# Second half of the query transposes moved within a turn: ahead of the last two gate/up groups and the tanh

## What is computed

```
x = x + tanh(g_xattn) * mlstm(q=layernorm(x), k=ctx, v=ctx)      # 16 heads of 64, scans of log gates
n = layernorm(x)
x = x + tanh(g_ffn) * (shared(n) + routed(n))                    # 16 experts, the best 2 of each token
shared(n) = (silu(n @ sg) * (n @ su)) @ sd
```

## Time and profile before

| | us |
|---|---|
| median of 3 runs | 2925.34 |
| lowest and highest run | 2923.26, 2928.15 |
| the profiled execution: its span, from the first to the last instruction | 2941.0 |

### The profile page before, as it was taken

How to read it: one execution, slowest core, us unless ns; L and a number is a source line. 1 busy time by engine, 2 the same in 40 slices (tenths; PEclk the granted TensorE clock), 3 DMA queues, 4 the chain that set the end, 5 groups by cost and what they waited for, 6 DMA issues and landing times.

```text
span 2941.0 us, 49274 instructions
## 1 busy us (share of the span) xinstructions
PE 2784.3 (95%) x17322; PEld 2290.3 (78%) x17323; DVE 1845.4 (63%) x2800; ACT 1015.8 (35%) x1948; POOL 996.6 (34%) x1148
## 2 busy tenths in 40 slices
PE   3799999999999986999999999999999999999999
PEld 2677777777777774788888888888888888888887
DVE  3787878878887854454555545545545546767676
ACT  4445444444444421233333333333333331111111
POOL 1334433434344423343343443443443411111111
PEclk7799999999999997999999999999999999999999
DMA  6445545554555541344444444443443327666665
GB/s 196 148 158 170 159 141 162 166 153 152 162 169 159 145 166 65 136 150 150 145 150 148 146 153 144 146 153 143 148 152 143 100 108 213 182 203 183 203 182 182
DMA packets 243470, 458.24 MB, mean 156 GB/s; under 512 B 99696, under 2 KB 131824, under 8 KB 240624
## 3 DMA queue, kind: packets, MB, share of 16 engines
q1 hardware_dynamic: 116976, 333.62, 33.9%
q0 software_dynamic: 34880, 73.10, 8.1%
q10 hardware_dynamic: 91488, 49.82, 6.3%
HBM read 358.96 MB, written 115.31 MB: 161 GB/s over the span
## 4 chain that ended last, share of the span: by engine, by line
PE 59%; DVE 1%; issue 0%; ACT 0%; DMA 0%; SPq 0%; ACTq 0%; DVEq 0%
PE p_g_b L1608 19%; PE p_up_b L1608 19%; PE p_y_b L1594 19%; PE p_h_b L1581 1%; DVE x_t_b L1473 0%; DVE w_lo L1439 0%; DMA xn<-mid_xn 0%; ACT w_hi L1361 0%; SPq L1204 0%; DVE xt_lo_b L1479 0%; ACT xt_hi_b L1394 0%; DVE th_b L1485 0%; DVE x L1515 0%; DVE x L1506 0%; DVE y_b L1517 0%
## 5 line engine op out<-in xcount | busy, mean ns | idle before, releaser
L1300 POOL DMA_INDIRECT xn<-mid_xn,idx_q x284 | 304.5, 1072 | 512.6 <-DVE x_t_b L1473 424.6
L1608 PE MATMUL p_g_b<-w_hi,xt_hi_b 128*128 128x512 f32 x840 | 334.6, 398 | 19.8 <-DVE xt_lo_b L1479 16.9
L1594 PE MATMUL p_y_b<-w_hi,ht_hi_b 128*128 128x512 f32 x840 | 327.4, 390 | 1.9 <-DVE ht_lo_b L1462 1.9
L1608 PE MATMUL p_g_b<-w_lo,xt_hi_b 128*128 128x512 f32 x840 | 328.6, 391 | 0.0
L1608 PE MATMUL p_g_b<-w_hi,xt_lo_b 128*128 128x512 f32 x840 | 328.4, 391 | 0.0
L1608 PE MATMUL p_up_b<-w_hi,xt_lo_b 128*128 128x512 f32 x840 | 328.0, 390 | 0.0
L1608 PE MATMUL p_up_b<-w_hi,xt_hi_b 128*128 128x512 f32 x840 | 327.8, 390 | 0.0
L1608 PE MATMUL p_up_b<-w_lo,xt_hi_b 128*128 128x512 f32 x840 | 327.7, 390 | 0.0
L1594 PE MATMUL p_y_b<-w_hi,ht_lo_b 128*128 128x512 f32 x840 | 327.5, 390 | 0.0
L1594 PE MATMUL p_y_b<-w_lo,ht_hi_b 128*128 128x512 f32 x840 | 327.4, 390 | 0.0
L1462 DVE TENSOR_TENSOR ht_lo_b<-p_h_b,ht_hi_b 128x512 fp32r<-128x512 f32 x74 | 51.0, 690 | 367.5 <-ACT ht_hi_b L1377 367.5
(11 more groups left out here) (224 smaller groups left out, 5585.8 us busy)
## 6 DMA issues: line engine op xcount, KB each, us to landing
mid_y<-y_b SPq DMA_DIRECT2D x73, 512.0 KB, 2.6
stage<-mid_g_row SPq DMA_DIRECT2D x64, 512.0 KB, 5.4
stage<-in_eg SPq DMA_DIRECT2D x16, 2048.0 KB
stage<-in_eu SPq DMA_DIRECT2D x16, 2048.0 KB
stage<-in_ed SPq DMA_DIRECT2D x16, 2048.0 KB
mid_y<-in_x SPq DMA_DIRECT2D x34, 512.0 KB
stage<-in_x SPq DMA_DIRECT2D x32, 512.0 KB
stage<-in_ctx_t ACTq DMA_DIRECT2D x32, 512.0 KB, 8.9
```

Of the source, the lines that this page charges most:

```text
L1300: nc.gpsimd.indirect_dma_start(out=xg_parts[:, n, :], out_offset=None, in_=xn_flat, in_offset=bass.IndirectOffsetOnAxis(ap=idx_q[:, n:n + ...
L1594: last = nc.tensor.matmul(p_y[n][:, :], a[:, k, :], b[:, GUP + k, w], start=(k == 0 and m == 0), stop=(k == FE // P - 1 and m == 2))
L1608: mm = nc.tensor.matmul(out[:, :], a[:, k, :], w[:, k, o:o + FE], start=(k == 0 and m == 0), stop=(k == KD - 1 and m == 2))
```

## The change

The step Q3 moves from the end of the tuple to the place between Z1 and U1. PE thus transposes the second half of the queries ahead of K7 and K8, and ACT copies it ahead of the tanh. Offsets, waits, tiles and all other steps stay as they are; the order of the steps that share `p_tr` among each other is the same.

```diff
                 "A9", "F2", "B4", "A7", "A8", "E3", "G2", "R1", "G3", "C1", "F3", "G4", "X1", "G5", "Q2", "C2", "G6",
-                "E4", "W6", "Z1", "U1", "D1", "K7", "K8", "Q3")
+                "E4", "W6", "Z1", "Q3", "U1", "D1", "K7", "K8")
```

## The result

| | median, us | lowest to highest | runs |
|---|---|---|---|
| before, beside the changed kernel | 2926.74 | 2923.26 to 2930.46 | 4 |
| after | 2941.71 | 2938.29 to 2943.12 | 4 |

The change makes the kernel slower: ratio 1.0048, 95% interval 1.0036 to 1.0060. The prediction, 2922.5 us with a range of 2909 to 2938, was wrong in sign and the time lies outside the range. It lies where the third rival put it (2939.9).

A forecast was written before the change was run, and what follows sets the result against it. PE, busy 95% of the span, was taken to bound the kernel. Terms -17.4 + 1.1 + 13.5 = -2.8 us, put on the runs' median of 2925.34 us, gave 2922.5 us, range 2909 to 2938.

The forecast's parts named there:

- the third rival: PE stops ahead of K7 for Q2's copy, DVE meets POOL just as often: +14.6 us, 2939.9 us; chance 0.20.
- The 17.4 us of irregular waits: PE's 19 waits for DVE at L988, L981 and L1044 in turns 2 to 29, all taken as going: -17.4 us.
- undisturbed turns: PE waits at A3 instead of A2 and is 0.04 us later at B2: +1.1 us over 28 turns.
- stops at L943: Ahead of K7, Q3's transposes wait for ACT's copy of Q2, which shares their PSUM buffer: 19 turns, +13.5 us.
- The gap at A2 isn't saved, it goes to A3: A2 starts earlier, but A3 needs L707 from the DVE chain: some 0.7 us wait there replaces 0.8 us at A2.
- B2 0.04 us later per turn: The second half of L1044 follows the second L762 and starts at 533.06 instead of 533.02 in turn 14.
- A new wait for ACT's copy: Q3's transposes at L943 wait for ACT's copy of Q2, up to 1.3 us each in 19 turns: 13.5 us.
- the slow side: Signs of a too low forecast: L943's waits add up to over 20 us, or L988's and L1044's stay at 11 us.
- The irregular waits go: The later DVE chain passes its collisions with POOL, so waits at L988, L981 and L1044 vanish: -17.4 us, the softest term.
- The first: Rival: the regular gap ahead of A2 is simply saved, 28 x 1.06 = 29.7 us, 2895.6 us; chance 0.06.
- The second, 2909 us: Rival: the irregular waits go and Q2's copy is in time, -16.3 us, 2909.0 us; chance 0.14.

The follow-up runs named there:

- the second profile of before: The kernel before, unedited, profiled anew on the same chip as the kernel after: 2925.58 us, profiled span 2925.1 us.
- the second profile of after: The kernel after, unedited, run on the same chip as the kernel before: 2938.85 us, 1.0044 times before.
- The kernel with the buffer: Order of the change, but Q3's transposes go into one of the two score buffers: 2929.83 us (0.9997 of before), on another chip 2928.68 us (0.9994).
- the trace of after that ran beside the buffer: The changed kernel, unedited, on the same chip as the second run with Q3's own buffer: 2937.77 us, 1.0028 of before.

## Why the prediction was wrong

The step that failed is the one that put the sum on the median: "the runs' median, 2925.34 us, is 15.7 us lower, and I put the difference on the median". The 17.4 us of irregular waits, taken as all going, were most of what made the profiled execution of before 15.7 us longer than the runs: the second profile of before has 12.9 us less of them, and 26 of its turns take 15.5 us less. That execution, which takes the usual time, has 4.5 us of them, so there the change has little to take away. On the median the term of -17.4 us was worth -3.9.

The account can be made from the starts of the tanh (L630) in turns 2 and 28, 26 turns apart, for the second profile of before:

```profile
136.49 0.60 ACT L630 ACTIVATE th<-p_g 128x512 f32<-128x512 f32 x1 [3.93 <-PE p_up L1006]
...
969.42 0.60 ACT L630 ACTIVATE th<-p_g 128x512 f32<-128x512 f32 x1 [1.98 <-PE p_up L1006]
```

and for after:

```profile
134.54 0.60 ACT L630 ACTIVATE th<-p_g 128x512 f32<-128x512 f32 x1 [2.07 <-PE p_up L1006]
...
980.50 0.60 ACT L630 ACTIVATE th<-p_g 128x512 f32<-128x512 f32 x1 [2.08 <-PE p_up L1006]
```

832.93 and 845.96 us: 13.0 us longer (845.75 us in the second profile of after, from the same chip as this one of before). The turns repeat in fours. Undisturbed ones are 31.51, 31.25, 32.66 and 32.29 us long before, and 31.68, 31.42, 32.89 and 32.45 us after. Turns with a stop, or with a wait at L988, are longer than their kind, and the excess is the price of the disturbance:

| over 26 turns, us | predicted (28 turns) | measured, against the usual execution of before |
|---|---|---|
| undisturbed turns | +1.1 | (31.68 + 31.42 + 32.89 + 32.45 - 127.71) / 4 x 26 = +4.7 |
| stops at L943 | +13.5 | +12.3, in 7 turns, of which 8.5 is idle time |
| irregular waits of before | -17.4 | -3.9, in 4 turns |
| sum | -2.8 | +13.1 |

In the first profile of before the same 26 turns take 848.4 us (134.98 to 983.36), 15.5 us more than in the second, so against that execution after is 2.4 us shorter; the sum said 2.8. The sum was thus about right for the execution that it was made on and wrong for the median. The prediction showed that gap of 15.7 us and even called the irregular waits its softest term, but it doubted whether the change would remove them, not whether the runs had them.

Step by step:

- *The gap at A2 isn't saved, it goes to A3.* Right: 28 waits of 0.75 us, predicted "some 0.7".
- *B2 0.04 us later per turn.* Right in sign, mis-sized: 0.15 us in turn 14, 0.18 us per turn. The prediction let B2's second half follow the second L762, 0.05 us behind its end, the step that it had read between L707 and L981. In the rows of after it is B2's first half that is held, and it starts 0.21 us behind the end of the first L762.
- *A new wait for ACT's copy, 13.5 us in 19 turns, with nothing to cover it.* The mechanism is right, and the runs with and without a shared buffer show it. The total came out near (12.3 us), its parts didn't. There are 7 stops, not 19 (8 and 9 in other profiles). A reading of this, which no run tests, is that a stop sets PE back against ACT, so that the turn behind it finds the copy in time: in after no stop follows directly on another, but in its second profile three do (turns 16 to 18). Instead one stop is long, 3.45 us against "up to 1.3", and costs 2.35 us more by the clock, so that the total is near by luck. L943's waits stayed under the 20 us that were to show the slow side.
- *The irregular waits go.* They are gone in after, as said, but there were few to go, and that the shift of 0.36 us takes them away isn't shown. The kernel with the buffer has the same shift without the stops, and its L989, which is L988 there, waits 4.3 and 3.8 us in the two traces, about as much as the 4.5 us of before. That POOL's L493 holds L707, as the prediction has it, fits the first profile (in the seven turns with a wait at L981, L707 starts 0.1 to 0.7 us behind the end of an L493), but no run tests it.
- *The gain of the other rivals.* The first fell with the 28 waits at A3. The second, 2909 us, fell with both: the copy isn't in time, and the waits to be removed weren't there. The third gave the time and named the right wait, but the half of it by which DVE meets POOL "just as often" isn't in the trace of after, which has no wait at L988 or L1044. Its time is right in part by luck: it counted 1.1 us for the undisturbed turns, which cost 4.7, and nothing for the waits that went, -3.9.

What stays open: why one turn of a run has a stop of over 3 us. In turn 24 ACT's exponentials waited for POOL's mask, and POOL for the broadcast of the gate row; each of the three profiles of after has one such stop (3.5, 3.2 and 3.3 us), and what delays the broadcast wasn't traced further. Nor was it found why executions of the kernel before differ by 16 us in how often DVE and POOL meet.

## What to carry to other kernels

When a step is moved forward on an engine that takes its work in order, look up what frees its buffer and how late that may come at the old place: the slack there is the real price, since everything queued behind pays for the wait, and here 1.4 us of products more or less decided between none and 8.5 us of stops. Before irregular waits of a profile are counted as gain, compare the profiled execution's time with the median of the runs; if it is longer by about as much as these waits sum to, they aren't the change's to remove. A regular gap ahead of one instruction is worth taking away only if the next thing that PE needs doesn't hang on the same event by another chain.

## What was not expected of the hardware

- A stop of 3.45 us of PE was followed by some 6 us at a granted clock of 0.50, 2.35 us lost on twelve products; after a stop of 1.79 us the clock stayed at 1.00. Two stops of nearly the same length differed in the trace of after that ran beside the buffer: one of 1.91 us ended at 327.36 us, PE was at work again, and the granted clock was 0.50 from 329 to 332 us; after one of 1.90 us, which ended at 852.62, it stayed at 1.00.
- The same program without any edit ran in two patterns: spans of 2941.0 and 2925.1 us, with 17.4 and 4.5 us of irregular waits of PE at the end of DVE's chains. The medians of the unedited kernel were between 2925 and 2933 us from one group of runs to the next.
